# Attention scores with keys on partitions, and probabilities as the stationary operand for V

## The chip, the cores and the metric

The kernel runs on one core of one Trainium2 chip. The metric is the device time of one execution in microseconds (us). The core has five engines that run their own instruction streams and meet at semaphores: TensorE (PE) multiplies, VectorE (DVE), ScalarE (ACT) and GpSimd (POOL) work on elements, SyncE (SP) issues most transfers.

## What is computed

One transformer layer on 2048 tokens of 512 features: attention with 8 heads of 64, a layer norm, a mixture of 64 experts (6 of them for a token) with a shared expert, and a second layer norm. The change is in the attention:

```python
q = x @ Wq + bq
k = x @ Wk + bk
v = x @ Wv + bv
q, k, v = (to_heads(q), to_heads(k), to_heads(v))       # 8 heads of 64
scores = jnp.einsum('bdsh,bdth->bdst', q, k) / SCALE    # SCALE = sqrt(8)
weights = jax.nn.softmax(scores, axis=-1)
feats = jnp.einsum('bdst,bdth->bdsh', weights, v)
x = _layernorm(x + (feats @ Wo + bo), axis=-1)
```

## The kernel before

Everything is fp32 outside. For TensorE a factor is split into a high part in the type fp32r, which goes through the array in one pass, and a low part, the rest. A product of two split factors is then made of several one-pass matmuls.

The prologue turns x, projects it to k, q and v, and keeps them split: `k_stack` (head's 64 rows of high and 64 of low part on 128 partitions, all 2048 keys), `v_pair` (tokens on partitions; for each head 64 columns high, 64 low), and q in HBM (`q_hbm`), from where each head's part comes back as `q_stack`.

Attention runs over 8 chunks of 256 queries and 8 heads: 64 pairs m of chunk and head, each of STEPS = 4 steps, so 256 steps. Every engine walks through the same loop over s by hand-written order (`for s in range(LAST + LAG + 2)`), and semaphores tie them. In one step:

- PE turns a quarter of the probabilities of step r = s - 6 (L1146): 4 key tiles x 2 query halves, 8 transposes of 128x128 into a PSUM slot, `turn`.
- PE makes the scores of step s (L1159), queries on partitions: for a query half and 1024 keys, 2 banks x 2 parts (q high and q low against `k_stack`), 4 matmuls of 512 columns.
- DVE scales the scores out of PSUM into `prob` and takes the row's extreme on the way (L940); ACT raises to the exponential in place with the row's extreme as bias, and sums the row (L687).
- ACT copies the turned probabilities out of PSUM to `p_hi` (L674, in two halves), and in every second step a half to `prob` (L676), from which POOL makes a quarter of the low parts `p_lo` (L514); DVE makes the others (L919).
- PE multiplies the step before with V (L1178): for 4 key tiles, `v_pair` is the stationary operand (128 columns, high and low V) and `p_hi`, then `p_lo`, the moving one of 256 columns: 8 matmuls into `pv_acc`.

At the end of a head the reciprocal row sums are spread by two transposes (L1188), the product is scaled by DVE (L927), the part from V's low columns is moved by a DMA (L401) to the other partitions and added by POOL (L530, `head_out` waits for it). At the end of a chunk a generator `chunk_end` on each engine is stepped twice a step by `side_step`, with `ticks` as its clock: output projection (L1092, plain fp32), residual and norm, turning x1 (L1101), the gate (L1108), ranks, and the scatter of rows to the experts' places (L472 on POOL). The steps at which the pieces are due are written as numbers (P0, P1).

Three PSUM slots of two banks serve the list `takes` in turn; a take waits for the reader of the third one before it (`wait_bank`). `misc` is a bank that small results share. After attention come the experts and the final weighted sum. Nothing there is changed but a few dues of the last chunk's end.

## Time and profile before

| | us |
|---|---|
| two runs, median (lowest to highest) | 1483.91 (1481.65 to 1486.16) |
| the profiled execution | 1479.0 |
| its span on the core | 1477.3 |
| prologue, to about | 157 |
| attention, 157 to about | 957 |
| experts and final sum, to | 1477 |

The profile counts an engine as busy while any of its instructions runs. For PE these overlap: a matmul's record includes its latency, so the pace is read from starts. PEld is the weight load, a record of its own.

### The profile page before, as it was taken

How to read it: one execution, taken by the hardware profiler on the slowest of the kernel's cores; microseconds unless marked ns; L12 is line 12 of the kernel's file. 1: busy time of each engine (PE TensorE's matmuls, PEld its weight loads, DVE VectorE, ACT ScalarE, POOL GpSimd, SP SyncE). 2: the span in 40 equal slices, each digit the busy share in tenths (PEclk: the TensorE clock that was granted, in tenths of full speed). 3: DMA queues.
4: the chain of work that ended last, by engine and by line, in shares of the span. 5: the costliest groups of instructions: out<-in, count | busy, mean ns of one | idle time of the engine just before them, and what ended most of it. 6: DMA issues, size and time to landing. Idle time of an engine off the chain costs nothing. (4 is left out here: it accounts for less than half of the span.)

```text
span 1477.3 us, 24021 instructions
## 1 busy us (share of the span) xinstructions
PE 1280.4 (87%) x8064; PEld 1068.7 (72%) x8064; DVE 1059.5 (72%) x1964; ACT 875.6 (59%) x1573; POOL 598.6 (41%) x588
## 2 busy tenths in 40 slices
PE   7999899999999999999999999869999999960000
PEld 6888799898898998998988989847666666630000
DVE  4523688799898897997988989746665656645665
ACT  4421589788787887886887868712555555530000
POOL 0002223245244344343443442523444444447785
PEclk9999999999999999999999999979999999985555
DMA  9998111122122122121221221246999999966665
GB/s 353 351 375 290 52 32 37 46 79 81 43 82 86 33 92 78 60 85 61 79 89 37 81 87 39 76 150 202 292 321 333 330 328 332 323 209 192 205 204 159
DMA packets 158374, 235.79 MB, mean 160 GB/s; under 512 B 14000, under 2 KB 102576, under 8 KB 158256
## 3 DMA queue, kind: packets, MB, share of 16 engines
q1 hardware_dynamic: 131920, 147.50, 31.9%
q0 software_dynamic: 24576, 83.88, 16.1%
q10 hardware_dynamic: 1760, 2.88, 0.6%
q8 instruction: 68, 1.11, 0.3%
q14 instruction: 50, 0.41, 0.1%
HBM read 118.89 MB, written 109.05 MB: 154 GB/s over the span
## 5 line engine op out<-in xcount | busy, mean ns | idle before, releaser
L674 ACT ACTIVATE p_hi<-slot 128x512 fp32r<-128x512 f32 x512 | 279.3, 596 | 108.3 <-PE slot L1146 98.8
L514 POOL TENSOR_TENSOR p_lo<-prob,p_hi 128x512 fp32r<-128x512 f32 x128 | 165.5, 1293 | 436.2 <-ACT prob L676 432.4
L1159 PE MATMUL slot<-k_stack,q_stack 128*128 128x512 f32 x1024 | 300.5, 416 | 4.5 <-POOL v_pair L455 4.5
L687 ACT ACTIVATE prob<-prob,row_min 128x1024 f32<-128x1024 f32 x256 | 296.3, 1158 | 8.6 <-DVE prob L940 8.6
L919 DVE TENSOR_TENSOR p_lo<-slot,p_hi 128x512 fp32r<-128x512 f32 x384 | 250.8, 681 | 44.0 <-ACT p_hi L674 42.6
L1178 PE MATMUL pv_acc<-p_hi,v_pair 128*128 128x256 f32 x1024 | 265.6, 292 | 3.8 <-POOL p_lo L514 3.2
L1146 PE MATMUL slot<-ident,prob 128*128 128x128 f32 x2048 | 265.2, 272 | 1.2 <-ACT prob L687 1.2
L1178 PE MATMUL pv_acc<-p_lo,v_pair 128*128 128x256 f32 x1024 | 255.2, 282 | 0.0
L1146 PEld LDWEIGHTS slot<-ident,prob 128*128 128x128 f32 x2048 | 230.9, 140 | 1.7 <-DVE prob L940 1.6
L1178 PEld LDWEIGHTS pv_acc<-p_hi,v_pair 128*128 128x128 f32 x1024 | 193.0, 189 | 17.9 <-issue 8.4
L1178 PEld LDWEIGHTS pv_acc<-p_lo,v_pair 128*128 128x128 f32 x1024 | 192.8, 188 | 11.7 <-issue 3.4
L1159 PEld LDWEIGHTS slot<-k_stack,q_stack 128*128 128x128 f32 x1024 | 174.8, 191 | 27.9 <-issue 4.9
L940 DVE TENSOR_SCALAR_CACHE_REDUCE prob<-slot,row_min 128x1024 f32<-128x1024 f32 x128 | 163.1, 1275 | 5.2 <-remote 4.7
L940 DVE TENSOR_SCALAR_CACHE_REDUCE prob<-slot 128x1024 f32<-128x1024 f32 x128 | 155.2, 1213 | 3.9 <-PE slot L1159 3.9
L964 DVE TENSOR_TENSOR rows_lo<-slot,rows_hi 128x1024 fp32r<-128x1024 f32 x72 | 88.1, 1224 | 96.7 <-ACT rows_hi L717 96.7
L1242 PE MATMUL slot<-down_w,hid 64*128 64x512 f32 x256 | 126.5, 615 | 0.0
L567 POOL DMA_INDIRECT got<-y_hbm,slot_of x96 | 106.8, 1113 | 31.7 <-issue 29.2
L1012 DVE SCALAR_TENSOR_TENSOR base<-got,weight_of,base 128x512 f32<-128x512 f32 x96 | 71.0, 751 | 60.6 <-DMA got<-y_hbm,slot_of 60.2
L472 POOL DMA_INDIRECT disp_hbm<-resid,scat x96 | 95.6, 996 | 32.8 <-issue 23.2
L1205 PEld LDWEIGHTS slot<-ident,rows 128*128 128x128 f32 x576 | 63.8, 144 | 61.2 <-DMA rows<-disp_hbm 45.1
L544 POOL TENSOR_TENSOR up_lo<-up_w,up_hi 128x512 fp32r<-128x512 f32 x64 | 80.7, 1262 | 67.0 <-ACT up_hi L721 67.0
L717 ACT ACTIVATE rows_hi<-slot 128x1024 fp32r<-128x1024 f32 x72 | 73.9, 1026 | 52.9 <-PE slot L1205 48.9
(133 smaller groups left out, 2041.7 us busy)
## 6 DMA issues: line engine op xcount, KB each, us to landing
disp_hbm<-zeros SPq DMA_DIRECT2D x64, 512.0 KB, 6.5
rows<-disp_hbm SPq DMA_DIRECT2D x64, 512.0 KB, 7.3
y_hbm<-y_out POOLq DMA_DIRECT2D x64, 512.0 KB, 7.1
q_stack<-q_hbm SPq DMA_DIRECT2D x128, 128.0 KB
up_w<-in_L_ffn_w_up SPq DMA_DIRECT2D x64, 256.0 KB, 4.4
down_w<-in_L_ffn_w_down SPq DMA_DIRECT2D x64, 128.0 KB, 5.2
stage<-in_L_attn_x SPq DMA_DIRECT2D x8, 512.0 KB, 9.4
q_hbm<-q_hi SPq DMA_DIRECT2D x8, 512.0 KB, 3.8
```

The lines of the kernel that those rows point to most:

```text
L472: e.indirect_dma_start(disp_hbm, bass.IndirectOffsetOnAxis(scat[:, k:k + 1], 0), resid[j][:, :], None, bounds_check=E * CAP - 1, oob_is_er ...
L514: e.tensor_tensor(p_lo[1][:, 2:4, :], prob[:, m % 2, :, (4 * u + 2) * P:(4 * u + 4) * P], p_hi[1][:, 2:4, :].bitcast(F32), ALU.subtract).t ...
L567: e.indirect_dma_start(got[use % NG][:, :], None, y_hbm, bass.IndirectOffsetOnAxis(slot_of[:, u, k:k + 1], 0), bounds_check=E * CAP - 1, o ...
L674: e.activation(p_hi[b][:, two, :], view[:, two, :], ACT.Copy).then_inc(a_phi, 1)
L687: e.activation(keys, keys, ACT.Exp, bias=row_min[:, me % 2, j, 1:2], scale=-1.0, accum_out=row_sum[:, me % 2, j, half:half + 1]).then_inc( ...
L919: e.tensor_tensor(p_lo[b][:, two, :], view[:, two, :], p_hi[b][:, two, :].bitcast(F32), ALU.subtract).then_inc(v_lo, 1)
L940: e.tensor_scalar(prob[:, ms % 2, j, half * HALF:(half + 1) * HALF], slot_of_take("scores", s)[:, :], -1.0 / SCALE, first, ALU.mult, ALU.m ...
L964: e.tensor_tensor(rows_lo[f % 2][:, :, :], slot_of_take("flip", f)[:, :].rearrange("p (k q) -> p k q", k=KC), rows_hi[f % 2][:, :, :].bitc ...
L1146: made = e.transpose(view[:, t, j * P:(j + 1) * P], prob[:, m % 2, j, (4 * u + t) * P:(4 * u + t + 1) * P], ident[:, :])
L1159: made = e.matmul(slot[:, n * BANK:(n + 1) * BANK], qs[:, part, j * P:(j + 1) * P], k_stack[:, ms % H, keys], start=part == 0, stop=part == 1)
L1178: made = e.matmul(pv_acc[:, 0:QC], v_pair[:, kt, mv % H, :], src[:, t, :], start=kt == 0 and part == 0, stop=kt == NT - 1 and part == 1)
L1242: made = e.matmul(slot[:, t * BANK:(t + 1) * BANK], hid[o][0:width, t * P:(t + 1) * P], weights[:, :], start=True, stop=True)
```

## The change

- **Scores with keys on partitions.** Step r's exact scores come straight in the layout that the turned probabilities had (`st` takes the place of `turn`, s - 6 as before): for each of 4 key tiles one matmul with 128 keys of `k_stack` (high and low) as stationary operand and `q_twice` (q high on both halves of the partitions) as moving one, 256 columns; and one with `k_one` (64 rows of k high and a row of ones) against `q_low` (64 rows of q low, and as the 65th row the negative row maximum).
- **The row maximum** comes from a product of its own, q high against `k_stack`, 2 matmuls of 512 columns (`max`), which DVE reduces (`tensor_reduce`) without writing the scores; the two halves are joined in `top_max`, turned by two transposes to a row, and ACT writes it negated into `q_low`.
- **Exponential**: ACT reads the slot of `st` and writes `prob` (128x1024, now two buffers of one step's size), copies it to `p_hi`; DVE and POOL make one half each of `p_lo` in every step.
- **V**: `p_hi` and `p_lo` are stationary (128 queries), V moves. `v_pair` has 130 columns a head: low V, two ones, high V. `p_hi` meets all 130 columns, `p_lo` the last 66; the ones give the row sums. 16 matmuls a step, two steps behind the scores (PLAG = 8).
- **End of a head**: ACT copies `pv_acc` (128x260), POOL takes the reciprocal by a power, adds the two parts and multiplies (`join`). The DMAs of `moved` and `feats` go. **End of a chunk**: the features have queries on partitions, so PE turns them (`turn_feats`, 4 transposes a tile) and ACT copies them before the projection; the dues move back (P0 from 14 to 20, P1 from 38 to 44).
- **Loads**: per head q high twice, q low once, and 64 rows of `k_stack` copied by DMA into `k_one`. The first of them stand behind `prologue_over`. POOL writes the ones into `v_pair` and `k_one`.

```diff
-        STEPS, LAG = 4, 6
+        STEPS, LAG, PLAG = 4, 6, 8
@@ sync: loads of a head
+            def load_q(m):
+                c, h = divmod(m, H)
+                if m >= NQ:
+                    e.wait_ge(p_st, 4 * (m - NQ) + 4)
+                src = q_hbm[h // 2, 0, (h % 2) * D:(h % 2 + 1) * D, c * QC:(c + 1) * QC]
+                for half in (slice(0, D), slice(D, P)):
+                    e.dma_start(q_twice[m % NQ][half, :].bitcast(F32), src).then_inc(d_q[m % NQ], 16)
+            def load_low(m):
+                c, h = divmod(m, H)
                 if m >= 2:
+                    e.wait_ge(p_st, 4 * (m - 2) + 4)
+                rows = slice((h % 2) * D, (h % 2 + 1) * D)
+                e.dma_start(k_one[m % 2][0:D, :].bitcast(F32),
+                            k_stack[rows, h, :].bitcast(F32)).then_inc(d_kone[m % 2], 16)
+                e.dma_start(q_low[m % 2][0:D, :].bitcast(F32),
+                            q_hbm[h // 2, 1, rows, c * QC:(c + 1) * QC]).then_inc(d_low[m % 2], 16)
+            prologue_over(e)
             load_q(0)
+            load_low(0)
             load_q(1)
-            prologue_over(e)
+            load_low(1)
...
@@ gpsimd
             prologue_over(e)
+            for b in range(2):
+                e.memset(k_one[b][D:D + 1, :].bitcast(F32), 1.0).then_inc(g_kone, 1)
...
+            def join(m):
+                h, out_cols = m % H, slice((m % H) * D, (m % H + 1) * D)
+                e.wait_ge(a_pv, m + 1)
+                e.tensor_tensor(pv_inv[:, :], pv_sb[:, :, D], minus_one[:, :].to_broadcast([P, QT]),
+                                ALU.pow).then_inc(g_inv, 1)
+                e.tensor_tensor(pv_sb[:, :, 0:D], pv_sb[:, :, 0:D], pv_sb[:, :, VW - D:VW], ALU.add).then_inc(g_join, 1)
...
+                e.tensor_tensor(feats[:, :, out_cols], pv_sb[:, :, 0:D],
+                                pv_inv[:, :].unsqueeze(2).to_broadcast([P, QT, D]), ALU.mult).then_inc(g_feat, 1)
...
+                    e.tensor_tensor(p_lo[r % NP][:, 2:4, :], prob[r % 2][:, 2:4, :],
+                                    p_hi[r % NP][:, 2:4, :].bitcast(F32), ALU.subtract).then_inc(g_lo, 1)
@@ scalar
+                if mv > 0 and uv == 0:
+                    e.wait_ge(p_pv, 4 * mv)
+                    e.wait_ge(g_feat, mv - 1)
+                    e.activation(pv_sb[:, :, :], pv_acc[:, 0:QT * VW].rearrange("p (j n) -> p j n", j=QT),
+                                 ACT.Copy).then_inc(a_pv, 1)
                 r = s - LAG
                 if 0 <= r < LAST:
+                    e.wait_ge(p_st, r + 1)
                     if r >= 2:
+                        e.wait_ge(v_lo, r - 1)
+                        e.wait_ge(g_lo, r - 1)
+                    e.activation(prob[r % 2][:, :, :], slot_of_take("st", r)[:, :].rearrange("p (t q) -> p t q", t=4),
+                                 ACT.Exp, scale=1.0 / SCALE).then_inc(a_exp, 1)
...
+                        e.activation(p_hi[r % NP][:, two, :], prob[r % 2][:, two, :], ACT.Copy).then_inc(a_phi, 1)
...
+                    e.activation(q_low[mt % 2][D:D + 1, :], misc[0:1, 0:QC], ACT.Copy, scale=-1.0).then_inc(a_top, 1)
@@ vector
+                    e.tensor_reduce(row_max[:, ms % 2, half, j:j + 1], slot_of_take("max", s)[:, :], AX.X,
+                                    ALU.max).then_inc(v_max, 1)
@@ tensor
-                    for t in range(4):
-                        for j in range(QT):
-                            made = e.transpose(view[:, t, j * P:(j + 1) * P],
-                                               prob[:, m % 2, j, (4 * u + t) * P:(4 * u + t + 1) * P], ident[:, :])
+                    for t in range(4):
+                        keys = slice((4 * u + t) * P, (4 * u + t + 1) * P)
+                        e.matmul(view[:, t, :], k_stack[:, m % H, keys], q_twice[m % NQ][:, :], start=True, stop=False)
+                        made = e.matmul(view[:, t, :], k_one[m % 2][0:D + 1, keys], q_low[m % 2][0:D + 1, :],
+                                        start=False, stop=True)
...
-                        for part in range(2):
-                            made = e.matmul(slot[:, n * BANK:(n + 1) * BANK], qs[:, part, j * P:(j + 1) * P],
-                                            k_stack[:, ms % H, keys], start=part == 0, stop=part == 1)
+                        made = e.matmul(slot[:, n * BANK:(n + 1) * BANK], q_twice[ms % NQ][:, j * P:(j + 1) * P],
+                                        k_stack[:, ms % H, keys], start=True, stop=True)
...
-                        for part, src in enumerate((p_hi[b], p_lo[b])):
-                            made = e.matmul(pv_acc[:, 0:QC], v_pair[:, kt, mv % H, :], src[:, t, :],
-                                            start=kt == 0 and part == 0, stop=kt == NT - 1 and part == 1)
+                        for j in range(QT):
+                            cols, at = slice(j * P, (j + 1) * P), j * VW
+                            e.matmul(pv_acc[:, at:at + VW], p_hi[b][:, t, cols], v_pair[:, kt, mv % H, :],
+                                     start=kt == 0 and j == 0, stop=False)
+                            made = e.matmul(pv_acc[:, at + D:at + VW], p_lo[b][:, t, cols],
+                                            v_pair[:, kt, mv % H, D:VW], start=False,
+                                            stop=kt == NT - 1 and j == QT - 1)
```

## Rows read from the trace of the kernel before

**Rows 1.** The page: busy us and share, slices, costliest groups (page's columns)
```profile
PE 1280.4 (87%) x8064; PEld 1068.7 (72%) x8064; DVE 1059.5 (72%) x1964; ACT 875.6 (59%) x1573; POOL 598.6 (41%) x588
...
PEclk9999999999999999999999999979999999985555
...
L514 POOL TENSOR_TENSOR p_lo<-prob,p_hi 128x512 fp32r<-128x512 f32 x128 | 165.5, 1293 | 436.2 <-ACT prob L676 432.4
...
L687 ACT ACTIVATE prob<-prob,row_min 128x1024 f32<-128x1024 f32 x256 | 296.3, 1158 | 8.6 <-DVE prob L940 8.6
...
L1146 PE MATMUL slot<-ident,prob 128*128 128x128 f32 x2048 | 265.2, 272 | 1.2 <-ACT prob L687 1.2
...
L1146 PEld LDWEIGHTS slot<-ident,prob 128*128 128x128 f32 x2048 | 230.9, 140 | 1.7 <-DVE prob L940 1.6
```

**Rows 2.** Windows, attention and its tail: busy (count), PEclk, DMA share, GB/s
```profile
157.00:957.00 800.00, 794.20 (x5552) 714.08 (x5552) 693.23 (x1420) 656.38 (x1244) 316.78 (x312) 1.00 0.20 66
958.00:1000.00 42.00, 26.43 (x122) 18.28 (x123) 16.59 (x42) 6.54 (x10) 13.97 (x16) 0.80 0.45 154
```

**Rows 3.** Timeline around one step: start, us from first start to last end
```profile
601.22 0.28 PE L1178 MATMUL pv_acc<-p_hi,v_pair 128*128 128x256 f32 x1
601.34 0.28 PE L1178 MATMUL pv_acc<-p_lo,v_pair 128*128 128x256 f32 x1
601.46 0.27 PE L1178 MATMUL pv_acc<-p_hi,v_pair 128*128 128x256 f32 x1
...
602.17 1.03 PE L1146 MATMUL slot<-ident,prob 128*128 128x128 f32 x8
...
602.87 1.09 ACT L674 ACTIVATE p_hi<-slot 128x512 fp32r<-128x512 f32 x2 [0.54 <-PE slot L1146]
...
602.96 1.17 PE L1159 MATMUL slot<-k_stack,q_stack 128*128 128x512 f32 x4
...
603.97 0.28 PE L1178 MATMUL pv_acc<-p_hi,v_pair 128*128 128x256 f32 x1
```

**Rows 4.** Timeline: four projection records, a gate, three of the gate's loads
```profile
466.81 1.95 PE L1092 MATMUL misc<-wo_sb,feats 128*128 128x512 f32 x4
...
425.69 1.00 PE L1108 MATMUL misc<-wg_sb,x_t 128*128 128x64 f32 x8
426.50 0.37 PE L1178 MATMUL pv_acc<-p_hi,v_pair 128*128 128x256 f32 x1
...
425.81 0.41 PEld L1108 LDWEIGHTS misc<-wg_sb,x_t 128*128 128x128 f32 x3
```

**Rows 5.** Single lines L1092 and L1108: duration ns min/median/max, first and last start
```profile
L1092 PE MATMUL misc<-wo_sb,feats x16: 592/592/667, 466.8 to 479.2; 128*128 128x512 f32 x16
...
L1108 PEld LDWEIGHTS misc<-wg_sb,x_t x8: 188/192/192, 425.5 to 426.4; 128*128 128x128 f32 x8
L1108 PE MATMUL misc<-wg_sb,x_t x8: 217/275/275, 425.7 to 426.4; 128*128 128x64 f32 x8
```

**Rows 6.** Timeline of the prologue's projections, 512 columns
```profile
60.20 0.40 PE L1032 MATMUL slot<-x_hi,w_hi 128*128 128x512 f32 x1
60.43 0.40 PE L1032 MATMUL slot<-x_lo,w_hi 128*128 128x512 f32 x1
```

**Rows 7.** Groups by form, ACT, 170 to 960 us
```profile
L694 ACT ACTIVATE scaled<-misc 128x256 f32<-128x256 f32 x64 | 25.0, 391 | 24.8 <-PE misc L1188 24.8
```

**Rows 8.** Groups by form, POOL, 170 to 960 us
```profile
L472 POOL DMA_INDIRECT disp_hbm<-resid,scat x80 | 79.1, 989 | 19.7 <-issue 19.2
...
L465 POOL TENSOR_TENSOR small<-small,half_neg 128x1 f32<-128x1 f32 x14 | 8.6, 611 | 0.0
```

**Rows 9.** Groups by form, POOL, prologue
```profile
L444 POOL MEMSET zeros<- 128x256 f32 x1 | 0.3, 302 | 0.0
```

**Rows 10.** DMA issues: count, KB each, median us to landing
```profile
resid<-in_L_attn_x SPq DMA_DIRECT2D x16, 256.0 KB, 2.8
```

**Rows 11.** The line of the q loads: issue ns min/median/max, first and last
```profile
L366 SPq DMA_DIRECT2D q_stack<-q_hbm x128: 573/612/1395, 135.8 to 918.1; - x128
```

More of the change, by code:

```diff
@@ L79, in build @@
         half_neg = sb("half_neg", [P, 1])
+        NP, NQ = 3, 3
+        minus_one = sb("minus_one", [P, 1])
         att = ExitStack()
@@ L185, in build @@
             "x_lo", "w_lo", "k_lo", "q_lo", "v_add", "v_lo"))
-        v_min, v_lo, v_sum, v_inv, v_scaled = (sem(f"dve_{n}") for n in ("min", "p_lo", "sum", "inverse", "scaled"))
+        v_max, v_lo, v_top = (sem(f"dve_{n}") for n in ("max", "p_lo", "top"))
         v_resid, v_norm = sem("dve_resid"), sem("dve_norm")
@@ L212, in build @@
         for s in range(LAST + LAG):
-            takes += ([("turn", s - LAG)] if s >= LAG else []) + ([("scores", s)] if s < LAST else [])
+            takes += ([("st", s - LAG)] if s >= LAG else []) + ([("max", s)] if s < LAST else [])
         for n in range(-2, NI):
@@ L531, in gpsimd @@
+                if s >= R1 + 3 and (s - R1 - 3) % 32 == 0:
+                    bias_resid((s - R1 - 3) // 32, 1)
+                if mv > 0 and uv == 0:
+                    join(mv - 1)
                 side_step(jobs)
@@ L538, in gpsimd @@
                 if n == -2:
+                    bias_resid(NCH - 1, 0)
+                    for _ in range(2 * SIDE):
+                        side_step(jobs)
                     bias_resid(NCH - 1, 1)
@@ L545, in gpsimd @@
                                     ALU.subtract).then_inc(g_wlo, 1)
-                for _ in range((3 if n == -2 else 1) * SIDE + SIDE):
+                for _ in range(2 * SIDE):
                     side_step(jobs)
```

331 lines of the change are left out of this document (151 added, 180 removed).

## The prediction

> **What bounds the kernel now.** I first read the busy table and the slices [rows 1]: TensorE (PE) is busy 87% of a span of 1477.3 us and its granted clock is at the upper level (2.4 GHz) in nearly all slices. Then I read the stretch that the change rewrites. Between 157 and 957 us PE is busy 794.2 of 800 us; VectorE (DVE) 693, ScalarE (ACT) 656 and GpSimd (POOL) 317 [rows 2]. So attention is 800 us and PE sets its end. Before it lies the prologue (157 us) and behind it the experts and the final sum (520 us); the change leaves both nearly alone. The question is: how long is PE's work for one step (a quarter of one head of one chunk; there are 8 x 8 x 4 = 256 steps)?
>
> The timeline of one step [rows 3] answers that. Starts count, because a matmul's own 0.28 to 0.60 us is mostly latency that overlaps the next one. The first probability product starts at 601.22 us, the transposes behind the eight products at 602.17, the four score matmuls at 602.96, the next products at 603.97. So: products 0.95, transposes 0.79, scores 1.01, together 2.75 us. Check: 256 x 2.75 = 704. Work at head and chunk ends: 16 output projections of 8 records, each record (1.95 - 0.59)/3 = 0.453, so 58 us [rows 4, 5]; 16 gates from 425.69 to 426.50, 13 us [rows 4]; 64 spreads of the reciprocals, two transposes each, and 16 x 4 transposes of x1, all at the 0.11 found below, 14 and 7 us. The sum is 796 of the 800 us.
>
> **Prices on PE.** An fp32r matmul of 512 moving columns follows its predecessor after 0.233 us [rows 6]; one of 256 after 0.119 [rows 3] (the starts at 601.22, 601.34, 601.46; over the whole group 0.95/8). The slope is 0.445 ns a column. But each matmul here also loads a stationary tile of 128 columns. With 128 moving columns the slope would give 0.057 us, and the trace shows (1.03 - 0.27)/7 = 0.11 between transposes [rows 1, 3]. The gate matmuls have 64 moving columns, and their loads stand (0.41 - 0.19)/2 = 0.11 apart [rows 4, 5]. Two widths, one pace: below some 250 moving columns the weight load sets the pace, at 0.110 us a pair.
>
> **The change, part by part, per step.**
> - Removed on PE: 8 transposes, 0.79, and 2 of the 4 score matmuls.
> - Kept in another role: the exact scores, now with keys as output partitions. 4 key tiles x 2 matmuls of 256 columns = 8 x 0.119 = 0.95.
> - The one-pass product for the row maximum: 2 matmuls of 512 columns, 2 x 0.233 plus the 0.07 that the first product behind them starts late now (1.01 - 4 x 0.233) = 0.54.
> - The product with V: the probabilities are now stationary. 4 key tiles x 2 query halves x 2 parts = 16 pairs, each with its own load, moving only 130 and 66 columns. By columns it is cheap (196 x 0.445 ns = 0.087 for two); by the load floor it is 16 x 0.110 = 1.76, against 0.95 now. I take the floor, since the nearest rows on both sides (64 and 128 columns) pay it. Bounds: 0.104 a pair (the eight gate matmuls by their starts, (1.00 - 0.275)/7 [rows 4, 5]) gives 1.66; 0.119 (as with 256 columns) gives 1.90.
> - Sum: 0.95 + 0.54 + 1.76 = 3.25 us a step, +0.50. Times 256: +128 us. Bounds +102 and +164.
>
> Loads per step go from 20 to 26 while moving columns fall from 5120 to 4640: the change saves what is not scarce.
>
> At the ends of heads, PE swaps two transposes for two (top maximum instead of reciprocals): 0. At chunk ends it adds four transposes of the features, 16 x 4 x 0.11 = 7, with entries and exits some 8 us.
>
> **The other engines** must fit in 3.25 us. ACT: an exp of 128x1024, 1.16 [rows 1], two p_hi copies 1.09 as a pair [rows 3], and per head two copies of at most 0.39, 0.2 a step [rows 7]: 2.45; with 0.15 for the new wait of the copies on the exp, 2.6. DVE: one half of p_lo a step instead of one and a half, and a maximum over 128x1024 in place of a pass of the same size that also wrote: less than now, and now it fits in 2.75. POOL: p_lo in every step instead of every second, 1.29 [rows 1], and three small operations per head. The power costs 0.61 as the root does [rows 8], the other two (128 elements a partition, a quarter of p_lo's 512) some 0.32 each: 0.31 a step, in all 1.60. All lie beside PE. POOL's scatters, about 1 us each [rows 8] and issued in pairs, and its waits on routing now sit in front of a p_lo that every product waits for; that product comes one step (3.2 us) later, which covers a pair. If the cover were gone it would cost up to 2 us, six times in each of 8 chunks, 96 us in all; by a slack of one step I put it at nothing. DMA: k_one needs 512 KB per head. A 256 KB load of x lands in 2.8 us [rows 10], so twice that size should in some 6; the wait behind which it is issued opens five steps (16 us) before its use, and in attention the DMA engines are 20% busy [rows 2]. q_twice is reloaded three steps ahead, and what it is queued behind on SP waits on earlier heads. The loads of x at chunk ends move back with the chunk's end and keep their distance. All hidden.
>
> The three PSUM slots: the maximum product of a step takes the slot whose exp was begun in the step before; it has a period for 1.1 us of exp. Hidden, as long as ACT stays at 2.6.
>
> **Start and end.** The first q load now stands behind the prologue's barrier, where before it was issued at 135.8 us, 20 us ahead: issue 0.6 x 2 [rows 11] and a landing as the 256 KB residual's 2.8 [rows 10] give 4. Beside it run two memsets of 2048 elements on one partition on POOL; one of 256 elements takes 0.30 [rows 9], so at most 2.4 each, 4.8 if nothing of it is fixed. So +4. At the end, the tail of the last chunk (PE busy 26 of 42 us from 958 to 1000 [rows 2]) gets the join, a turn and a flip, about 1.3 (above), 0.7 (four transposes) and 0.6 (a copy of p_hi's half size), and one more step of pipeline: +5.
>
> **The sum** against the profiled execution's own 1479.0 us: 1479 + 128 + 8 + 4 + 5 = 1624. The two runs' median is 1483.9, 0.3% higher; I predict 1625. With the bounds of the pair (-26, +36) and a few us of stalls, its own range is 1590 to 1680.
>
> **Rivals.**
> - *Narrow fp32r streams run like full fp32.* No row of before shows an fp32r matmul under 256 moving columns. Full fp32 is in the trace: a 512 column product is two records of 0.453 [rows 4, 5], 0.91, four times 0.23. If the 130 and 66 columns went at that rate, they would take 4 x 196 x 0.445 ns = 0.349 for two, 8 x 0.349 = 2.79 instead of 1.76: +264 us more, 1888. For it: 256 is the narrowest width anywhere. Against it: 256 and 512 show one slope and no step between. Chance 0.27. Here the Trainium skill ("FP8 and Floating Point Precision", section "TensorE Precision Notes") speaks against it: reduced precision reads the fp32 number and truncates it, and only true fp32 takes four passes; it names no width. No run here shows it yet.
> - *Delays instead of work*: ACT's chain, the slot ring or POOL's scatters cost PE 0.2 to 0.5 us a step. 1680 to 1750. Against it: the slack above. Chance 0.13.
> - *The loads hide better than the transposes show.* A load then costs little and 130 and 66 columns go by columns: 8 x 0.087 = 0.70, PE 2.19, and ACT's 2.45 binds: -0.30 x 256 = -77, with +17 at the ends 1419, **faster** by 4%. It decides once a pair costs under (2.75 - 0.95 - 0.54 - 0.07)/16 = 0.075 us. For it: a transpose's load takes 140 ns [rows 1] and the gate's 190 [rows 5], so these differ, and neither is an fp32r load. Against it: both keep the pace of 0.11 all the same. Chance 0.04.
> - *The loads hide in part*: a pair costs what its two matmuls do by columns, 0.087 (the lower end of what rows allow for one that has to load at all). Sixteen take 1.39, the step 2.88, and the time is 1479 + 33 + 17 = 1529; down to 0.075 a pair the change costs nothing. Against it: both narrow rows. Chance 0.03. The Trainium skill ("TensorE: Matmul & The Clock Gate", section "Back-to-back issue gap") has a rule near this: in a stream, a load and a matmul of 128 columns together take about 81 ns. By it the time would be an estimated 1506 us (sixteen pairs 1.30, a step 2.79). The trace disagrees at that very width, with 0.11.
>
> **Numbers.** Load floor 0.53, narrow streams as full fp32 0.27, delays 0.13, hidden loads 0.04, half-hidden 0.03. To leave out no more than 2 in 10, the range must take in the second: 1590 to 1890; if I leave it out, the likeliest alone is 1590 to 1680. By 2%, about what a measurement of this kernel can tell from no change: slower 0.94, same 0.02, faster 0.04.
>
> **What would show it.** In the profile after: sixteen products a step (first to last start) in about 1.75 us, loads 0.11 apart, a step of 3.25, PE still 99% busy in attention, ACT near 75%, attention about 935 us long. If the products stand 0.23 and 0.12 apart alternately, it is the first rival. If PE has gaps in front of the maximum product or of the V product, the second. If two products start within 0.09, the third. What would make me most wrong is the width rule, which I read from matmuls of another type.

## The result and the profile after

The changed kernel takes 1617.33 us (median, 1615.92 to 1618.73) against 1483.91: a ratio of 1.0899, 95% interval 1.0817 to 1.0981. It is slower by 9%; 1625 was predicted. The profiled execution took 1615.9 us, with a span of 1614.2.

The page after: busy time, slices of the span, and the groups that answer to those of [rows 1] (out<-in, partitions x elements, count | busy us, mean ns of one | idle time before it and its releaser).

```profile
PE 1404.3 (87%) x9664; PEld 1214.3 (75%) x9664; DVE 1007.5 (62%) x1452; ACT 839.8 (52%) x1269; POOL 878.9 (54%) x855
...
PE   7997999999999999999999999987999999990000
...
PEclk9999899999999999999999999988999999995555
...
L534 POOL TENSOR_TENSOR p_lo<-prob,p_hi 128x512 fp32r<-128x512 f32 x256 | 372.1, 1455 | 240.2 <-ACT p_hi L715 239.4
L1202 PE MATMUL pv_acc<-v_pair,p_hi 128*128 128x130 f32 x2048 | 467.9, 302 | 0.5 <-POOL p_lo L534 0.5
L1204 PE MATMUL pv_acc<-v_pair,p_lo 128*128 128x66 f32 x2048 | 462.7, 245 | 0.0
L959 DVE TENSOR_REDUCE row_max<-slot 128x1 f32<-128x1024 f32 x256 | 312.5, 1222 | 223.1 <-PE slot L1185 215.4
L1202 PEld LDWEIGHTS pv_acc<-v_pair,p_hi 128*128 128x128 f32 x2048 | 392.1, 191 | 12.3 <-issue 4.0
...
L706 ACT ACTIVATE prob<-slot 128x1024 f32<-128x1024 f32 x256 | 262.6, 1026 | 232.2 <-PE slot L1173 177.9
L715 ACT ACTIVATE p_hi<-prob 128x512 fp32r<-128x512 f32 x512 | 294.9, 623 | 8.1
```

ScalarE and VectorE wait for PE (178 us and 215 us of their idle time), GpSimd for ScalarE (239 us). PE waits once at its start (8.5 us) and after that, up to its last product with V, 1.7 us in all: 0.5 for `p_lo` and 1.2 for `top_max`. The windows of the stretch that answers to [rows 2] say the same: PE 793.46 of 800 us, as full as before, and now full until 1078 us, not 958.

```profile
core 0: us, PE busy (x) PEld busy (x) DVE busy (x) ACT busy (x) POOL busy (x), PEclk, DMA share, GB/s
157.00:957.00 800.00, 793.46 (x6182) 742.02 (x6183) 560.07 (x783) 537.30 (x813) 512.13 (x489) 0.99 0.32 84
```

The timeline of one step (start, us from first start to last end) answers to [rows 3]:

```profile
602.31 0.22 PE L1202 MATMUL pv_acc<-v_pair,p_hi 128*128 128x130 f32 x1
602.38 0.24 PE L1204 MATMUL pv_acc<-v_pair,p_lo 128*128 128x66 f32 x1
602.45 0.31 PE L1202 MATMUL pv_acc<-v_pair,p_hi 128*128 128x130 f32 x1
602.60 0.25 PE L1204 MATMUL pv_acc<-v_pair,p_lo 128*128 128x66 f32 x1
602.67 0.31 PE L1202 MATMUL pv_acc<-v_pair,p_hi 128*128 128x130 f32 x1
...
604.01 0.36 PE L1172 MATMUL slot<-q_twice,k_stack 128*128 128x256 f32 x1
604.22 0.28 PE L1173 MATMUL slot<-q_low,k_one 65*128 65x256 f32 x1
604.34 0.29 PE L1172 MATMUL slot<-q_twice,k_stack 128*128 128x256 f32 x1
...
605.06 0.64 PE L1185 MATMUL slot<-k_stack,q_twice 128*128 128x512 f32 x2
605.54 0.22 PE L1202 MATMUL pv_acc<-v_pair,p_hi 128*128 128x130 f32 x1
```

Sixteen products with V take 602.31 to 604.01, 1.70 us; the exact scores 1.05; the product for the maximum 0.48. The step is 3.23 us where it was 2.75. Two products (130 and 66 columns) take 0.22 us, two times the pace of 0.11 that the prediction read for a load, and not the 0.087 us of 196 columns. The starts themselves stand 0.15 and 0.07 apart in turn, so it is the distance over two products that says what a product costs.

All stage lengths below run from the start of the first product with V to the start of the last one. By this measure the stage took 787.3 us before (170.3 to 957.6) and takes 902.7 us now (175.9 to 1078.5).

### The profile page after: what moved, and what is told of

It reads as the page before. It is cut to its first block and busy times, and to the rows that moved or that the text cites. A ratio compares the mean times of both kernels' runs of the same rounds, so it can differ in the third digit from the quotient of the medians.

```text
span 1614.2 us, 26847 instructions
## 1 busy us (share of the span) xinstructions
PE 1404.3 (87%) x9664; PEld 1214.3 (75%) x9664; DVE 1007.5 (62%) x1452; ACT 839.8 (52%) x1269; POOL 878.9 (54%) x855
## 5 line engine op out<-in xcount | busy, mean ns | idle before, releaser
L534 POOL TENSOR_TENSOR p_lo<-prob,p_hi 128x512 fp32r<-128x512 f32 x256 | 372.1, 1455 | 240.2 <-ACT p_hi L715 239.4
L1202 PE MATMUL pv_acc<-v_pair,p_hi 128*128 128x130 f32 x2048 | 467.9, 302 | 0.5 <-POOL p_lo L534 0.5
L1204 PE MATMUL pv_acc<-v_pair,p_lo 128*128 128x66 f32 x2048 | 462.7, 245 | 0.0
L959 DVE TENSOR_REDUCE row_max<-slot 128x1 f32<-128x1024 f32 x256 | 312.5, 1222 | 223.1 <-PE slot L1185 215.4
L1202 PEld LDWEIGHTS pv_acc<-v_pair,p_hi 128*128 128x128 f32 x2048 | 392.1, 191 | 12.3 <-issue 4.0
L1204 PEld LDWEIGHTS pv_acc<-v_pair,p_lo 128*128 128x128 f32 x2048 | 392.4, 192 | 11.2 <-issue 3.3
L706 ACT ACTIVATE prob<-slot 128x1024 f32<-128x1024 f32 x256 | 262.6, 1026 | 232.2 <-PE slot L1173 177.9
L715 ACT ACTIVATE p_hi<-prob 128x512 fp32r<-128x512 f32 x512 | 294.9, 623 | 8.1
L1172 PE MATMUL slot<-q_twice,k_stack 128*128 128x256 f32 x1024 | 280.3, 304 | 0.0
L1173 PE MATMUL slot<-q_low,k_one 65*128 65x256 f32 x1024 | 259.8, 285 | 0.0
L946 DVE TENSOR_TENSOR p_lo<-prob,p_hi 128x512 fp32r<-128x512 f32 x256 | 212.9, 832 | 21.9 <-ACT p_hi L715 20.1
```

The costliest lines, as they stand in the source:

```text
L534: e.tensor_tensor(p_lo[r % NP][:, 2:4, :], prob[r % 2][:, 2:4, :], p_hi[r % NP][:, 2:4, :].bitcast(F32), ALU.subtract).then_inc(g_lo, 1)
L706: e.activation(prob[r % 2][:, :, :], slot_of_take("st", r)[:, :].rearrange("p (t q) -> p t q", t=4), ACT.Exp, scale=1.0 / SCALE).then_inc( ...
L715: e.activation(p_hi[r % NP][:, two, :], prob[r % 2][:, two, :], ACT.Copy).then_inc(a_phi, 1)
L946: e.tensor_tensor(p_lo[r % NP][:, 0:2, :], prob[r % 2][:, 0:2, :], p_hi[r % NP][:, 0:2, :].bitcast(F32), ALU.subtract).then_inc(v_lo, 1)
L959: e.tensor_reduce(row_max[:, ms % 2, half, j:j + 1], slot_of_take("max", s)[:, :], AX.X, ALU.max).then_inc(v_max, 1)
L1172: e.matmul(view[:, t, :], k_stack[:, m % H, keys], q_twice[m % NQ][:, :], start=True, stop=False)
```

## The experiments

Times below are medians; the kernel before ran beside each on the same chip at 1482.3 to 1484.3 us. Line numbers in profiles of experiments shift by a few. A "step" is from the first product with V to the next step's first, or, where PE also waits, the usual distance between undisturbed steps.

### 1. More columns for the low part

```diff
-                            made = e.matmul(pv_acc[:, at + D:at + VW], p_lo[b][:, t, cols],
-                                            v_pair[:, kt, mv % H, D:VW], start=False,
+                            made = e.matmul(pv_acc[:, at:at + VW], p_lo[b][:, t, cols],
+                                            v_pair[:, kt, mv % H, :], start=False,
```

> The changed kernel, but the low probabilities also meet all 130 columns of V instead of the last 66 (the extra part is low times low and harmless). Theory (the weight load sets the pace of a narrow pair, 0.11 us at any width up to some 250 columns): 16 pairs stay at 1.70 us a step, the time stays at 1617 within 6. Rival (a matmul costs its columns, 0.445 ns each, above a fixed part): 8 x 64 x 0.445 ns = 0.23 us a step more, 1675.

Measured: 1611.31 us, ratio 1.0869 [1.0845, 1.0893], step 3.22. Half of the products move 130 columns in place of 66 and no product gets longer:

```profile
602.48 0.28 PE L1202 MATMUL pv_acc<-v_pair,p_hi 128*128 128x130 f32 x1
602.59 0.28 PE L1204 MATMUL pv_acc<-v_pair,p_lo 128*128 128x130 f32 x1
602.70 0.27 PE L1202 MATMUL pv_acc<-v_pair,p_hi 128*128 128x130 f32 x1
```

The stage takes 903.6 us, 902.7 in the changed kernel. Up to 130 columns at least, columns are free. The 6 us by which the whole is shorter don't lie in the stage but behind it, where the two kernels have the same code: 526.7 us from the last product's start to the end of the span, 535.7 in the changed kernel.

### 2. 256 columns for both parts

```diff
-                            cols, at = slice(j * P, (j + 1) * P), j * VW
-                            e.matmul(pv_acc[:, at:at + VW], p_hi[b][:, t, cols], v_pair[:, kt, mv % H, :],
+                            cols, at = slice(j * P, (j + 1) * P), j * 256
+                            col0 = (kt * H + mv % H) * VW
+                            wide = min(256, NT * H * VW - col0)
+                            e.matmul(pv_acc[:, at:at + wide], p_hi[b][:, t, cols], v_flat[:, col0:col0 + wide],
...
-                            made = e.matmul(pv_acc[:, at + D:at + VW], p_lo[b][:, t, cols],
-                                            v_pair[:, kt, mv % H, D:VW], start=False,
+                            made = e.matmul(pv_acc[:, at:at + wide], p_lo[b][:, t, cols],
+                                            v_flat[:, col0:col0 + wide], start=False,
```

> The changed kernel, but both products with V move 256 columns (the head's 130 and whatever lies behind them, which goes to unused PSUM columns; the result is not touched). Theory (load floor, and at 256 columns the 0.119 us of the old products): 16 x 0.119 = 1.90 instead of 1.70 a step, +51 us, 1668. Rival (columns count): (1024 - 392) x 4 / 2 = 2528 extra columns a step at... worked out for 8 couples: (512 - 196) x 8 x 0.445 ns = 1.12 us a step, +288, 1905.

Measured: 1641.80 us, 1.1069 [1.1043, 1.1095]. The rival's 1905 is far off. The size was missed too: 25 us more than the changed kernel where 51 were expected; the stage alone is 32 us longer (934.4 us). The sixteen products do take 1.89 us (602.05 to 603.94), 0.118 each, but the exact scores behind them shrink from 1.05 to 0.96 (603.94 to 604.90): behind a narrow product the first two score matmuls start 0.20 to 0.21 apart, behind one of 256 columns 0.12 to 0.13. The step is 3.33.

### 3. The low part as bf16 stationary

```diff
+        none_bf = sb("none_bf", [P, D + 2], BF16)
...
-        p_lo = [sb(f"p_lo{i}", [P, 4, QC], F32R, att) for i in range(NP)]
+        p_lo = [sb(f"p_lo{i}", [P, 4, QC], BF16, att) for i in range(NP)]
...
-                                            v_pair[:, kt, mv % H, D:VW], start=False,
+                                            none_bf[:, :], start=False,
```

> The changed kernel, but the low probabilities are written in bf16, and the 66 columns that they meet are bf16 zeros. Left out: the low part of the product with V. Count and shapes of the matmuls stay. Theory (the load of the stationary tile sets the pace; the rank matmuls' bf16 load took 95 to 101 ns where fp32 and fp32r loads take 188): a low product falls from 0.11 to 0.03 to 0.06 us, the step by 0.4 to 0.64, 1455 to 1515. Rival (a fixed price per matmul or per instruction, whatever the type): 1617.

Measured: 1557.71 us, 1.0512 [1.0481, 1.0543], step 2.94. That is 60 us under the changed kernel and still above the expected 1455 to 1515. The same sixteen loads of 128 columns, eight of them of another type, and the step is 0.29 us shorter. PE's timeline:

```profile
600.77 0.22 PE L1204 MATMUL pv_acc<-v_pair,p_hi 128*128 128x130 f32 x1
600.84 0.20 PE L1206 MATMUL pv_acc<-none_bf,p_lo 128*128 128x66 bf16 x1
600.88 0.31 PE L1204 MATMUL pv_acc<-v_pair,p_hi 128*128 128x130 f32 x1
601.02 0.21 PE L1206 MATMUL pv_acc<-none_bf,p_lo 128*128 128x66 bf16 x1
601.06 0.31 PE L1204 MATMUL pv_acc<-v_pair,p_hi 128*128 128x130 f32 x1
```

Two products take 0.187 us instead of 0.222. The number of moving columns was left alone and the pace changed, so something that goes with the type of the low product sets it. The record of its load is 97 ns long on average in place of 192. Load and moved zeros changed type together, and every matmul in this kernel has a load of its own, so no run parts the load from a fixed price of an fp32r product. That it is the load is the likelier reading, not a shown one; the price per product, and that columns up to 130 don't enter it, are shown. The saving was smaller than expected: of the two distances between starts the one behind the low product fell from 0.07 to 0.04, the other stayed at 0.14 to 0.15.

### 4. No low part at all

```diff
-                            e.matmul(pv_acc[:, at:at + VW], p_hi[b][:, t, cols], v_pair[:, kt, mv % H, :],
-                                     start=kt == 0 and j == 0, stop=False)
-                            made = e.matmul(pv_acc[:, at + D:at + VW], p_lo[b][:, t, cols],
-                                            v_pair[:, kt, mv % H, D:VW], start=False,
-                                            stop=kt == NT - 1 and j == QT - 1)
+                            made = e.matmul(pv_acc[:, at:at + VW], p_hi[b][:, t, cols], v_pair[:, kt, mv % H, :],
+                                            start=kt == 0 and j == 0, stop=kt == NT - 1 and j == QT - 1)
```

> The changed kernel without the products of the low probabilities (left out: 8 of the 16 matmuls with V a step, and with them the row sums of the low part). p_lo is still made. Theory: PE falls by 0.85 to 2.38 us a step, then ScalarE with 1.03 + 1.15 + 0.2 = 2.4 and its waits binds, so 2.4 to 2.55: 1405 to 1445. Rival (PE's load is not what sets the step, but the chain of exp, copies and low parts): less than 60 us of gain, above 1555.

Measured: 1494.32 us (ten executions, 1482.8 to 1509.5), 1.0055 [1.0024, 1.0087], where 1405 to 1445 was expected. Undisturbed steps are 2.33 us, 0.9 less, which is what eight products of 0.11 take; but the median step is 2.69. PE now waits 29 us for GpSimd's p_lo (33 times), 18 us for VectorE's top maximum and 12 for VectorE at the chunk ends. The granted clock adds to this. It is 0.94 over the stage, where it falls nine times behind a wait of 1.3 to 1.4 us, and once more at the end. One of these waits, 1.42 us for `top_max`, ends at 405.47. The window behind it (columns as above) has a granted clock of 0.57:

```profile
406.00:418.00 12.00, 12.00 (x60) 11.09 (x60) 8.35 (x12) 6.90 (x11) 4.46 (x5) 0.57 0.28 62
```

With half of the V products gone, attention is no longer PE's alone.

### 5. The V part of the change alone

The kernel before, with probabilities stationary and v_pair moving; its scores, transposes and row minimum stay. What follows the product is left as it was and mixes the queries up, so the output is wrong while the work is the same.

```diff
-                        for part, src in enumerate((p_hi[b], p_lo[b])):
-                            made = e.matmul(pv_acc[:, 0:QC], v_pair[:, kt, mv % H, :], src[:, t, :],
-                                            start=kt == 0 and part == 0, stop=kt == NT - 1 and part == 1)
+                        for j in range(QT):
+                            cols, at = slice(j * P, (j + 1) * P), j * P
+                            e.matmul(pv_acc[:, at:at + P], p_hi[b][:, t, cols], v_pair[:, kt, mv % H, :],
+                                     start=kt == 0 and j == 0, stop=False)
+                            made = e.matmul(pv_acc[:, at:at + D], p_lo[b][:, t, cols],
+                                            v_pair[:, kt, mv % H, 0:D], start=False,
+                                            stop=kt == NT - 1 and j == QT - 1)
```

> The kernel before, with only the product with V turned round: the probabilities are stationary, V moves with 128 columns against the high and 64 against the low part, 16 matmuls a step instead of 8 (the result then lies with queries on partitions and the code behind it mixes it up: the attention's output is garbage, all instructions stay). Theory: the V part alone costs (16 x 0.11 - 0.95) = +0.75 to 0.80 us a step, 1479 + 200 = 1670 to 1695; the scores part of the change, which is missing here, is worth -0.27 a step (1.52 instead of 1.80), -69. Rival (the new scores part is what costs, through k_one's transfers, the extra reduction or the slots): this one is near 1484 to 1550.

Measured: 1679.03 us, 1.1328 [1.13, 1.1355], step 3.56.

```profile
600.59 1.09 PE L1146 MATMUL slot<-ident,prob 128*128 128x128 f32 x8
601.44 1.17 PE L1159 MATMUL slot<-k_stack,q_stack 128*128 128x512 f32 x4
602.45 0.22 PE L1179 MATMUL pv_acc<-v_pair,p_hi 128*128 128x128 f32 x1
...
604.15 0.55 PE L1146 MATMUL slot<-ident,prob 128*128 128x128 f32 x3
```

The sixteen products take 1.70 us (602.45 to 604.15), as in the changed kernel. So the V part costs 0.81 us a step, and the scores part must give back 3.56 - 3.23 = 0.33. The stages say nearly the same: 985.1 us here, 902.7 in the changed kernel, 787.3 before, which is 0.77 up and 0.32 down a step. That pointed to the next kernel: keep the gain, leave the loss.

### 6. The scores part alone

The changed kernel with V stationary again, as before. A head's result is turned by two transposes and copied by VectorE so that `join` fits, the chunk end is due six turns later, and the low part of each head's last feature is left out.

```diff
-                            e.matmul(pv_acc[:, at:at + VW], p_hi[b][:, t, cols], v_pair[:, kt, mv % H, :],
...
-                            made = e.matmul(pv_acc[:, at + D:at + VW], p_lo[b][:, t, cols],
...
+                        for part, src in enumerate((p_hi[b], p_lo[b])):
+                            made = e.matmul(pv_acc[:, 0:QC], v_pair[:, kt, mv % H, :], src[:, t, :],
```

> The changed kernel's scores with the old product: V stationary again (64 high columns, one column of ones, 63 low columns: the low part of the last feature of each head is left out, since 129 columns do not fit), the probabilities moving with 256 columns. The 128x256 result is turned by two transposes per head so that the changed kernel's join and chunk end fit. Theory: step 0.96 + 0.57 + 0.95 = 2.48 us against 3.23 and 2.75; attention 917 - 192 + 20 = about 745; total 1448, range 1430 to 1480, faster than both kernels. Rival (ScalarE at 2.45 plus waits, or VectorE with one more copy, binds at 2.7 and more): 1500 or above.

Measured: 1591.53 us, 1.0724 [1.0692, 1.0757]: far from 1448. The undisturbed step is 2.37 to 2.40, just as the sum of its parts says, and yet the time is 7% above before. PE is busy 691 of 797 us, at a granted clock of 0.95. The waits between 160 and 900 us (us in total, times, longest) begin with GpSimd's for the x rows:

```profile
ACT prob L707 <- POOL p_lo L536: 77.8, 19, 6.9
...
POOL resid L468 <- DMA resid<-in_L_attn_x: 54.8, 12, 6.2
...
PE pv_acc L1208 <- POOL p_lo L536: 39.3, 18, 3.9
```

GpSimd adds the output bias to the x rows in the same queue as p_lo, and SyncE issues the load of these rows behind other work of its own (its queue waits 634 us in all for PE's scores, ahead of loads of q). While GpSimd waits for them, p_lo is late, and ScalarE and PE with it.

### 7. The x rows loaded a chunk earlier

Four buffers for x rows in place of two, their bias ahead of the scatters, scatters one in a step, chunk-end work on other steps; two buffers for p_lo in place of three pay for the room.

```diff
-        R0, R1 = LAG + PLAG + 28, LAG + PLAG + 33
+        L0, L1, B0, B1 = 37, 40, 41, 43
...
-                e.dma_start(resid[j][:, :], x_tiles[c * QT + j])
+                e.dma_start(resid[c % 2 * QT + j][:, :], x_tiles[c * QT + j])
```

> The mixed kernel of the run before this one (scores as in the change, V as in the kernel before, with the low part of the last feature of each head left out of V), with its attention stage made to wait less: the two x rows of a chunk are loaded one chunk ahead into buffers of their own (four in place of two), their bias is added on GpSimd before the scatters rather than behind them, the scatters go out one in a step, not two in every second step, the head's turned sums are joined one step later, and the single transposes of a chunk end stand on other steps than the transposes of a head. Two buffers for p_lo in place of three pay for the room. Work is the same. Theory (the mixed kernel's undisturbed step of 2.40 us is the price of its TensorE work, and what it lost above that went into waits that begin with GpSimd's wait for the x rows, 69.0 us in 15 waits, and go on as late p_lo, 93.7 us on ScalarE and 48.5 us on TensorE): 1460 us, between 1435 and 1500, with GpSimd's wait for the x rows under 10 us. Rival (VectorE and GpSimd slow each other whenever they overlap and bound the stage at about 2.85 us a step whatever the order): 1560 to 1600, with TensorE's waits for p_lo as large as before. If the mixed kernel is under 1470, it beats both the kernel before and the changed one.

Measured: 1550.03 us, 1.0449 [1.0427, 1.0471]. GpSimd's wait for the x rows is nearly gone (4.8 us between 160 and 957), and the whole is 41 us shorter. The theory was right about that wait and wrong that it was the whole. GpSimd also waits for earlier V products now, through the third buffer given up, 38.9 us, mostly covered: PE's own wait for p_lo fell from 48.5 us to 22.3. What was left is seen around 430 us: first VectorE, then PE, then the windows of the two stretches.

```profile
430.67 1.19 DVE L942 TENSOR_TENSOR p_lo<-prob,p_hi 128x512 fp32r<-128x512 f32 x1
431.79 1.21 DVE L949 TENSOR_TENSOR top_max<-row_max 128x2 f32<-128x2 f32 x1
```

```profile
427.53 0.28 PE L1168 MATMUL slot<-q_twice,k_stack 128*128 128x256 f32 x1
427.64 0.28 PE L1169 MATMUL slot<-q_low,k_one 65*128 65x256 f32 x1
...
428.50 0.63 PE L1181 MATMUL slot<-k_stack,q_twice 128*128 128x512 f32 x2
...
433.05 0.59 PE L1208 MATMUL misc<-ident,top_max 128*1 128x128 f32 x2 [2.98 <-DVE top_max L949]
433.29 0.56 PE L1168 MATMUL slot<-q_twice,k_stack 128*128 128x256 f32 x1
433.65 0.41 PE L1169 MATMUL slot<-q_low,k_one 65*128 65x256 f32 x1
433.86 0.42 PE L1168 MATMUL slot<-q_twice,k_stack 128*128 128x256 f32 x1
...
435.14 1.05 PE L1181 MATMUL slot<-k_stack,q_twice 128*128 128x512 f32 x2
```

```profile
420.00:430.00 10.00, 10.00 (x77) 9.42 (x75) 9.90 (x16) 9.24 (x15) 5.65 (x6) 1.00 0.34 75
430.00:440.00 10.00, 7.01 (x34) 6.26 (x34) 7.21 (x11) 3.82 (x7) 4.94 (x5) 0.66 0.28 64
```

The top maximum handles two numbers a partition and stands behind p_lo on VectorE; PE waits 2.98 us for it. Then the granted clock is 0.66 on average over that window: matmuls start 0.214 apart in place of 0.120, which is the lower level (1.2 GHz) for some 6 us. The eight exact scores take 1.85 us (433.29 to 435.14) where they took 0.97 (427.53 to 428.50). With the maximum product (0.86 for 0.46), the V products (1.85 for 0.96) and part of the next scores it comes to 2.6 us. This wait of 3 us costs nearly 6.

### 8. The same work in another order

On VectorE the maximum stands straight behind the reduction that it needs, ahead of the next p_lo; on GpSimd the scaling of a head's features gets a function of its own, called one step later. VectorE's p_lo also goes ahead of its share of the chunk end, and several dues of the chunk end move by one or two turns; the run doesn't part these.

```diff
-                mt, ut = divmod(s - STEPS, STEPS)
+                mt, ut = divmod(s - STEPS + 1, STEPS)
...
+            def scale_feats(m):
+                h, out_cols = m % H, slice((m % H) * D, (m % H + 1) * D)
...
+                if mv > 1 and uv == 0:
+                    scale_feats(mv - 2)
```

> The mixed kernel with the freed buffers of the run before this one (1550.03 us), in another order; the work is the same, and as there the low part of the last feature of each head is left out of V. VectorE takes the maximum over a row's two halves (top_max) straight after the reduction it needs, not behind the next p_lo and a share of the chunk end; it does p_lo ahead of its first share of the chunk end; GpSimd scales a head's features one step after joining them, so that the first head of a chunk doesn't wait for the turn of the chunk before it, and counts the ranks a step later; the single transposes and matmuls of the chunk end stand on steps with no other use of their PSUM bank. Theory (in the run before this one TensorE stood for 77 us in three waits, for top_max 46.6 us, for GpSimd's p_lo 18.6 and for the normalized rows 11.4, each wait of about 3 us followed by some 6 us in which matmuls of 256 columns start 0.214 us apart in place of 0.120, granted clock 0.66 to 0.83 in those stretches, 0.95 over the stage, so that the waits cost about 41 us a second time): 1455 us, between 1430 and 1490, with a mean granted clock of at least 0.98 in the stage. Rival (VectorE with 85% of the stage and its overlaps with GpSimd is the bound, and a wait removed comes back at the next instruction): 1520 to 1550. Under 1470 it beats both the kernel before and the changed one.

Measured: 1482.07 us, 0.9995 [0.9981, 1.0008]. 68 us less than the run before, for order alone. The mean granted clock from 160 to 957 us is 0.99 (0.95 in 6 and 7), and the stage takes 771.9 us where the kernel before takes 787.3. Yet it is no faster than before as a whole, and above the expected 1455. Two things take the rest. One is VectorE: 34 us of PE's waits between 160 and 957 us end on it, and while routing runs it is busy 59.35 of 60 us:

```profile
415.00:475.00 60.00, 55.21 (x406) 50.32 (x406) 59.35 (x81) 48.17 (x74) 50.30 (x49) 1.00 0.40 111
```

There VectorE's operations get longer while GpSimd works beside them. Both timelines show it, an operation of 384 elements in 2.80 us while GpSimd does two p_lo in 2.54 (GpSimd pays nothing here, 1.27 is its usual time):

```profile
448.78 2.80 DVE L866 TENSOR_TENSOR x_t<-iota_e,small 128x384 f32<-128x384 f32 x1
451.50 0.41 DVE L941 COPY pv_sb<-misc 128x256 f32<-128x256 f32 x1
451.84 0.68 DVE L947 TENSOR_TENSOR p_lo<-prob,p_hi 128x512 fp32r<-128x512 f32 x1
```

```profile
448.61 2.54 POOL L528 TENSOR_TENSOR p_lo<-prob,p_hi 128x512 fp32r<-128x512 f32 x2
```

In run 7 the same operation took 1.11 us at 426.57, and in the changed kernel, at 606.88, 0.55. So the rival of this run is right in part, though its 1520 to 1550 is far off. The other is the end, from the last product's start to the end of the span: 533.2 us against 519.7. The changed kernel has 535.7.

### 9 and 10. The end of the kernel

The changed kernel and run 8 with one constant changed; in the second the last chunk's scatters go out back to back as well.

```diff
-        AHEAD, CLEAR, SIDE, K_ROUTE = NB - 1, NCH - 1, 4, 18
+        AHEAD, CLEAR, SIDE, K_ROUTE = NB - 1, NCH - 1, 6, 18
```

> The changed kernel with one number changed: behind the last attention step, a shared expert's block gives six turns to the last chunk's end work where it gave four (SIDE 6 for 4). Nothing is left out. From the last product with V to the first matmul of a routed expert the changed kernel needs 84.4 us, the kernel before 76.8. Theory (the list of turns of a chunk's end is six turns longer in the changed kernel, at about 1.2 us each, and its last ranks come at 55.6 us in place of 48.1): the last ranks come under 50 us after the last product, the first routed expert under 79, and the time is 1610 us, between 1606 and 1613. Rival (the chain of the last routing steps, each waiting on the one before, sets it, not the turns): 1617, last ranks at 55 us as before. The other 6 us by which the end grew lie in the routed experts, where the DMA share is 1.01; neither theory has them change.

> The reordered mixed kernel (1482.07 us, scores as in the change, V as before with the low part of the last feature of each head left out) with the same edit, six turns for four, and with the scatters of the last chunk issued back to back. Its profiled attention, from the first product with V to the last, took 771.9 us against 787.4 of the kernel before, and its end, from the last product on, 535.1 against 521.1. Theory (turns): its end shortens by 8 to 10 us, 1473 us (1468 to 1477), 0.6% under the kernel before. Rival (the chain of routing steps): 1482.

Measured: 1613.85 us, 1.0864 [1.0847, 1.088], and 1485.41 us, 1.0013 [0.9999, 1.0027]. The last ranks do come earlier in the first of them (48.8 us behind the start of the last product with V, 55.1 in the changed kernel), but the first routed expert still starts at 84.2 us in both, 83.9 in the changed kernel. The turns theory falls, and with it the hope of a version under both.

What is known of the 16 us by which the end is longer in the changed kernel's profile: 7.7 arise before the first routed expert, where PE now waits for VectorE's routing (4.08, 2.61 and 2.19 us in three places); 5.6 arise in the experts, whose work on PE is the same (263.3 us in 270 of after, 264.0 in 265 of before) at a DMA share of 1.01 (1.02 before), and 2.7 in the final sum. These 16 us aren't a constant. Runs 1 to 4 have the same code behind the last product, and there the end took 526.7, 530.4, 526.9 and 529.3 us; the code of before took 519.7 and, in run 5, 523.4. So the change costs 3 to 16 us at the end, from one profiled execution to the next. The first routed expert started at 78.3 to 81.6 us in runs 1 to 4, so that its 84.2 in run 9 is a weak test of a few us. The granted clock of that stretch differs too: 0.91 in run 1, 0.86 in the changed kernel, 0.82 in run 9, where PE waits less. Why the experts' transfers end later, and what holds the shared experts once the ranks are early, stays open.

## Why the prediction was right, and where it wasn't

**The V products.** 16 x 0.110 = 1.76 was the term that carried the answer. Measured: 1.70, 0.106 a product, inside its bounds of 0.104 and 0.119. Its reason (the load sets the pace below some 250 columns, read from transposes and gates of another type) was tested by changing width alone (66 to 130: nothing; to 256: 0.118), the number of products (run 4: 0.9 a step less for eight fewer) and the type of the low product, load and moved columns together (bf16: 0.29 a step less). That the price goes by products and not by columns is shown; that it is the load's is the likelier reading. The doubt it named last, the width rule, is settled for the widths tried: 66 and 130 columns of fp32r have no dearer rate. One of its signs needs care: single starts do stand within 0.09 us (0.07 behind each product of 66 columns), which it gave as the mark of hidden loads, but the next one then stands 0.15 away, and two take 0.22. The rule of the Trainium skill ("FP8 and Floating Point Precision", section "TensorE Precision Notes"), that only true fp32 takes four passes, agrees with the runs at 66, 130 and 256 columns. The other rule weighed ("TensorE: Matmul & The Clock Gate", section "Back-to-back issue gap"), 81 ns for a load with its matmul, doesn't: the runs show 106 to 112 ns with fp32r loads. Even a bf16 load beside an fp32r one took 0.187 us for two, 0.094 each.

**The exact scores and the maximum.** 0.95 was 1.05: the first two matmuls behind a narrow product start 0.21 apart, 0.09 more than the others, an entry that the sum had not charged here. 0.54 was 0.48: the late start of 0.07 that it charged to the product behind the scores [rows 3] isn't there. It was misread. The scores of before, split up, show where the 0.07 was:

```profile
602.96 0.47 PE L1159 MATMUL slot<-k_stack,q_stack 128*128 128x512 f32 x1
603.28 0.39 PE L1159 MATMUL slot<-k_stack,q_stack 128*128 128x512 f32 x1
```

The first score matmul, behind the narrow transposes, takes 0.31 us to the next start in place of 0.23, and the product behind the fourth is not late. So it is one entry, behind narrow matmuls, that the sum put at the wrong place: it is paid now where the exact scores follow the products with V. Runs 2 and 6, with 256 columns there, don't have it. The two terms together were forecast at 1.49 and are 1.53; with -0.06 at V the step comes to 3.23 where 3.25 was forecast.

**Attention as a whole.** From the first to the last product with V it took 902.7 us, 115 more than the 787.3 of before. The prediction had 128 + 8. The undisturbed steps give 0.48 x 256 = 123, and with the 8 us for the turned features 131 should stand there. Some 5 of the missing 16 are at the ends of heads, which the prediction set equal: there two transposes took 0.22 us before and now 0.14, 64 times. Nearly 3 are at the features' turns: 56 of them stand in the stage, at 0.09 us each, and take 5 us and not 8. Most of the rest is in the step. 0.48 was read from steps that nothing disturbs. Counted from start to start over the whole stage, with late starts behind other work and short waits, PE's three parts of a step take 2.82 us before and 3.27 after. That is 0.44 more and not 0.48, some 9 us over the 256 steps.

**Start and end.** The first score matmul started 4.2 us later than before; +4 was predicted, by the memset of k_one's rows and the late q load. PE waited 8.5 us there for k_one, 4.5 before for v_pair. The first product with V started 5.6 us later. The end was forecast at +5 (its own parts, 1.3, 0.7, 0.6 and a step of 3.25, add up to nearly 6) and cost +16 in this profile, 7 to 11 in those of runs 1 to 4. This term was too small: the prediction counted the join and one step of pipeline and not the waits on routing nor the experts' transfers. By the two profiles 115 + 6 + 16 = 137 stands against the 145 of the sum: the stage came out 21 us under its forecast, start and end 13 above. The range would have held without this; that the time lies within 8 us of the forecast is in part luck.

**The other engines.** ScalarE is busy 67% of the stage where 75% was forecast, in part since its exp from PSUM without a sum takes 1.03 us and not 1.16, in part since the average step, with the ends of heads and chunks, is 3.5 us long and not 3.25; VectorE fell from 693 to 560 us, as it should [rows 2]. GpSimd's p_lo takes 1.46 us on average instead of 1.29 [rows 1]. "The loads of x at chunk ends keep their distance" was wrong. GpSimd waits for them in the profile after:

```profile
ACT prob L706 <- POOL p_lo L534: 43.0, 19, 5.9
...
POOL resid L466 <- DMA resid<-in_L_attn_x: 33.0, 7, 5.6
```

It cost nothing (PE waited 0.5 us for p_lo), because a PE step of 3.23 us covers it. Run 6 shows what it costs once PE is down to 2.4, where PE waits 48.5 us for p_lo (29.3 in run 4): "hidden" was true for this step length alone. The rival of delays was rightly put low, for this kernel, not for those near it.

## What to carry to other kernels

Count the stationary loads, not only the moving columns: before turning a product round, compare loads per step (26 against 20 here, where every matmul has one), and let the operand with fewer tiles be stationary. Price the two halves of a change apart; here one half gained 0.33 us a step and the other lost 0.81. And when a change makes the bounding engine faster, expect waits for others to come up at once, and to cost up to nearly double where the clock falls with them: run 6 ended 144 us above the sum of its steps, and buffers and order alone (runs 7 and 8) brought back 109 of them.

## What was not expected of the hardware

- The granted clock falls behind single waits of PE. In run 7 it falls to its lower level (1.2 GHz) sixteen times in the stage, behind waits of 2.5 to 3.0 us and for some 3 to 7 us each (0.214 us between products of 256 columns in place of 0.120), and three such waits aren't followed by a fall. The length of the wait alone doesn't decide: in run 4 it falls nine times behind waits of 1.3 to 1.4 us, while others of 1.3 to 2.5 us aren't followed by a fall, and in run 8 twelve waits of 1.0 to 1.2 us aren't either. Over the stage the mean granted clock is 0.94 in run 4, 0.95 in run 7 and 1.00 in run 8.
- VectorE and GpSimd lengthen each other's operations. In run 7 p_lo on VectorE took 0.68 us at 434.18 and 1.19 at 430.67, while two p_lo on GpSimd took 2.94; the maximum of two numbers a partition took 1.21 in the same stretch. The comparison of 128x384 took 0.55, 1.11 and 2.80 in three kernels. Sorted by overlap, in the changed kernel and runs 7 and 8: VectorE's p_lo never took more than 0.74 us where no operation of GpSimd ran beside it (145 of them) and up to 3.4 us where it did; the maximum of two numbers 0.16 against up to 1.27; GpSimd's p_lo 1.26 to 1.29 against up to 1.83. The reductions out of PSUM took 1.20 to 1.23 us either way. VectorE's p_lo in the kernel before, which reads PSUM too, took 0.69 us at most, with GpSimd beside it or not.
- Products with a stationary operand of 128 columns keep a pace of 0.106 to 0.112 us between fp32r products, whether these move 66 or 130 columns; with 256 columns it is 0.118.
